# Block 2 of a two-block cross-attention kernel: keys and values from split operands, a later output product, and a second set of banks for some pairs

## What is computed

```python
# block 1
x1 = layernorm(x + mha(x, x, Wq1, Wk1, Wv1, causal=True))        # keys past a counted length are masked
x2 = layernorm(x1 + mha(x1, context, Wq2, Wk2, Wv2, causal=False))
h  = layernorm(x2 + (relu(x2 @ fc1_w.T + fc1_b) @ fc2_w.T + fc2_b))
# block 2
q, k, v = h @ wq + bq, context @ wk + bk, context @ wv + bv      # 16 heads of 64
scores = q @ k.T / 8 + fside + fside                             # fside: (32, 16, 64, 64)
out = layernorm(softmax(scores) @ v @ wo + bo + h)
```

## Time and profile before

| | |
|---|---|
| time, median of 3 runs | 393.7 us (392.85 to 400.62) |
| the profiled execution | 397.58 us |
| its span, first to last instruction | 395.4 us |
| mean granted TensorE clock | 0.956 |
| TensorE matmul busy | 345.0 us (87%) |
| VectorE / ScalarE / GpSimd busy | 293.4 / 232.7 / 235.7 us |
| DMA | 17.86 MB, mean 45 GB/s |

### The profile page before, as it was taken

One profiled execution on the slowest core, in us unless ns is written; L12 is line 12 of the kernel. 1 busy time (PEld: TensorE's weight loads), 2 busy tenths in 40 slices (PEclk: granted clock), 3 DMA queues, 4 the chain that ended last, 5 costly groups with the idle time before them and its releaser, 6 DMA issues.

```text
span 395.4 us, 13051 instructions
## 1 busy us (share of the span) xinstructions
PE 345.0 (87%) x5296; PEld 240.2 (61%) x5296; DVE 293.4 (74%) x833; ACT 232.7 (59%) x561; POOL 235.7 (60%) x372
## 2 busy tenths in 40 slices
PE   2868979899999999999999999999999978776644
PEld 1434535658686868585858586868675747364533
DVE  3554793897989898979797989797979675735141
ACT  1314625485858686767677676768685837363421
POOL 0135161658485858585858585858686665665361
PEclk9968889999999999999999999999999999999955
DMA  5991000010001010102020202020202020101000
GB/s 163 325 342 48 0 2 2 2 55 3 2 2 61 5 61 3 61 2 61 5 61 4 61 2 61 5 61 2 61 5 61 2 61 2 61 2 61 8 8 7
DMA packets 13178, 17.86 MB, mean 45 GB/s; under 512 B 1600, under 2 KB 10176, under 8 KB 13120
## 3 DMA queue, kind: packets, MB, share of 16 engines
q1 hardware_dynamic: 13120, 17.04, 13.9%
HBM read 15.99 MB, written 1.05 MB: 43 GB/s over the span
## 4 chain that ended last, share of the span: by engine, by line
PE 73%; POOL 8%; DVE 7%; ACT 6%; issue 4%; DMA 1%; SPq 1%; POOLq 0%; ACTq 0%; DVEq 0%
PE C_E L455 8%; PE C_E L537 7%; PE C_E L488 6%; PE C_E L469 6%; PE C_E L514 4%; PE C_E L528 4%; PE A_E L365 4%; PE C_E L503 3%; PE B_E L365 3%; PE A_E L398 2%; PE B_E L398 2%; PE B_E L384 2%; POOL B_kblk L888 2%; PE B_X L384 2%; PE A_X L384 2%
## 5 line engine op out<-in xcount | busy, mean ns | idle before, releaser
L568 ACT ACTIVATE A_S<-A_S 128x512 f32<-128x512 f32 x32 | 20.2, 631 | 65.8 <-DVE A_S L766 65.8
L888 POOL TENSOR_TENSOR A_kblk<-A_qk,cst 128x1024 f32<-128x1024 f32 x16 | 30.4, 1898 | 41.1 <-DVE A_qk L734 39.8
L896 POOL TENSOR_TENSOR L_ve<-L_mv,cst 128x1 f32<-128x1 f32 x64 | 12.3, 192 | 61.4 <-DVE L_mv L799 61.3
L929 POOL TENSOR_TENSOR Sc<-Sc,mxc 128x512 f32<-128x512 f32 x32 | 33.4, 1044 | 22.2 <-DVE mxc L846 22.2
L907 POOL TENSOR_TENSOR L_xg<-L_xh,vec_sb 128x128 f32<-128x128 f32 x64 | 29.4, 459 | 17.9 <-DVE L_xh L808 17.9
L898 POOL TENSOR_TENSOR L_rstd<-L_ve,cst 128x1 f32<-128x1 f32 x64 | 35.2, 551 | 5.0
L537 PEld LDWEIGHTS C_E<-wo_sb,C_zT 128*128 128x128 f32 x256 | 31.4, 200 | 11.1 <-ACT C_zT L633 11.1
L537 PE MATMUL C_E<-wo_sb,C_zT 128*128 128x128 f32 x256 | 34.6, 291 | 3.5 <-ACT C_zT L633 3.5
L455 PE MATMUL C_E<-cTs,wk_sb 128*128 128x512 f32 x64 | 36.0, 645 | 0.3 <-DVE Sc L837 0.3
L938 POOL TENSOR_TENSOR Pc<-Pc,rdc 128x512 f32<-128x512 f32 x32 | 33.0, 1045 | 4.8 <-DVE rdc L856 4.8
L646 ACT ACTIVATE qT<-C_E,bq 128x128 f32<-128x128 f32 x128 | 34.8, 384 | 0.7 <-PE C_E L488 0.7
(11 more groups left out here) (148 smaller groups left out, 954.5 us busy)
## 6 DMA issues: line engine op xcount, KB each, us to landing
f<-in_fs SPq DMA_DIRECT2D x16, 512.0 KB, 4.1
out<-osb SPq DMA_DIRECT2D x16, 64.0 KB, 2.0
xTs<-in_xT SPq DMA_DIRECT2D x1, 768.0 KB, 8.7
xs<-in_x SPq DMA_DIRECT2D x1, 768.0 KB, 10.7
cs<-in_ctxn SPq DMA_DIRECT2D x1, 768.0 KB, 12.4
cTs<-in_ctxT SPq DMA_DIRECT2D x1, 768.0 KB, 9.8
vec_sb<-in_vecs SPq DMA_DIRECT2D x1, 640.0 KB, 6.9
wk_sb<-in_wk SPq DMA_DIRECT2D x1, 512.0 KB, 4.3
```

What stands on the lines that cost most here:

```text
L888: tt(a.kblk[:], a.qk[:, 1].unsqueeze(1).to_broadcast([P, 8, P]), at["rmask"].unsqueeze(2).to_broadcast([P, 8, P]), ALU.mult).then_inc(a.s_ ...
L929: tt(v, v, mxc[:, 8 * g:8 * g + 8].unsqueeze(2).to_broadcast([P, 8, S]), ALU.subtract).then_inc(C.s_sub, 1)
```

## The change

1. **Split keys, values.** The context (`cT_hi`, `cT_lo`, for four pairs at a time) and the weights (`wk_hi`, `wk_lo`, `wv_hi`, `wv_lo`) are split: `hi` is a copy in the type F32R, `lo` is what is left. Keys and values are each three products with F32R operands in place of the f32 ones: hi by hi, lo by hi, hi by lo. The values are now two products' worth of 512 columns over all 128 tokens of the pair, and no longer go by sequence. New steps make the halves: `C.whi`, `C.wvhi`, `C.chi` on ScalarE, `C.wlo`, `C.wvlo` on VectorE, `C.clo` on GpSimd.
2. **Scores and bias.** In `C.e` the bank now goes by sequence `b`, and the partition half by `hl ^ b`. The bias arrives sorted to match (`by_half`, on the host), and `C.fadd_g` adds it once, reading four head pairs across both banks. The factor 2 moves: queries are scaled by half (`QSCALE`), and exp has `scale=2.0`.
3. **Delayed output product.** `C.o` is one step and comes after the next pair's scores and their sum with the bias. `C.e` waits for the copies `C.zts` of the pair before it and no longer for `C.y`.
4. **Two places.** From pair 12 (`SPLIT`) the odd pairs of block 2 use the E and X banks of chain A, which has then done its last pair, and its buffers. `place(n)` gives the set, `before(n)` the pair that had it before.
5. **Blank products.** `idle_products` multiplies zeros (bf16, 512 columns) into B's X bank: 7 at the start, 2 in each of 16 steps `K.warm` ahead of B's first scores, 3 in each of 16 steps `L.warm` after B's last norm, the last seven of these after the last output product.
6. **Order.** `MOVES` gives each step of each pair a shift of its own, so that periods need no longer have one order. In the middle the order on TensorE is, for example: `C.pt`(3) `A.qkv`(9) `C.zt`(3) `B.e`(6) `B.f1`(5) `C.e`(4) `A.pt`(8) `C.o`(3) `B.pt`(6) `C.k`(8) `C.v`(5) `B.tr`(7) `C.x3t`(5) `C.q`(5) `A.e`(9). Before it was `C.pt`(3) `C.zt`(3) `A.e`(8) `C.o`(3) `A.qkv`(9) `C.e`(4) `B.e`(6). The first order on ScalarE is `A.qk`(0) `C.whi`(0) `A.exp_0`(0). At the end TensorE has `C.x3t`(15) `C.q`(15) `C.pt`(14) `C.e`(15) `C.zt`(14), four blank steps, `C.o`(14), then `C.pt`(15), `C.zt`(15) and `C.o`(15) with three blank steps between them, and seven more.
7. The GpSimd step `gb` also waits for its own instruction of the pair before.

```diff
+QSCALE = 0.5 * float(DK1) ** -0.5
...
+def by_half(fs):
+    f = fs.reshape(PAIRS, 2, J, 2, S, S)
+    halves = [np.stack([f[:, b, :, c ^ b] for b in range(2)], axis=2) for c in range(2)]
+    return np.stack(halves, axis=1).transpose(0, 1, 4, 2, 3, 5).reshape(B * S, H * S)
...
-            a.J, a.E, a.X = ps(name + "_J"), ps(name + "_E"), ps(name + "_X")
+            a.J, a.EE = ps(name + "_J"), ps(name + "_E", 2)
+            a.E, a.X = a.EE[:, 0:HALF], a.EE[:, HALF:2 * HALF]
...
-        C.E = [ps("C_E0"), ps("C_E1")]
+        C.EE = ps("C_E", 2)
...
+        cT_hi, cT_lo = ([sb(f"{n}{k}", [P, FIRST * P], F32R) for k in range(2)] for n in ("cT_hi", "cT_lo"))
+        wk_hi, wk_lo, wv_hi, wv_lo = (sb(n, [P, HD], F32R) for n in ("wk_hi", "wk_lo", "wv_hi", "wv_lo"))
...
+        own = [Chain(), Chain()]
+        for k, o in enumerate(own):
+            o.EE = (C.EE, A.EE)[k]
+            o.E = [o.EE[:, b * HALF:(b + 1) * HALF] for b in range(2)]
+            o.S = A.S if k else sb("Sc", [P, H * S])
+            o.P = A.S if k else sb("Pc", [P, H * S])
+            o.PT = A.PT if k else sb("PTc", [P, H * S])
+            o.qT = A.kblk if k else sb("qT", [P, J, P])
+            o.zT = (wk_sb if k else sb("C_zT", [P, HD]))[:].rearrange("p (j b c) -> p j b c", b=2, c=S)
+            o.x3T = sb(f"x3T{k}", [P, P])
+            o.mx, o.den, o.rd = (sb(f"C_{nm}{k}", [P, H]) for nm in ("mx", "den", "rd"))
+
+        def place(n):
+            return own[n % 2 if n >= SPLIT else 0]
+
+        def before(n):
+            if n <= SPLIT:
+                return n - 1
+            return n - 2 if n > SPLIT + 1 else -1
...
+            def idle_products(to, count):
+                for _ in range(count):
+                    last = mm(to, blank[:, 0:P], blank[:], start=True, stop=True)
+                return last
+
+            def warm_first(n):
+                idle_products(Bc.X[:, :], 2).then_inc(warmed, 1)
+
+            def warm_last(n):
+                pe.wait_ge(L2.s_xh, PAIRS)
+                idle_products(Bc.X[:, :], 3)
...
+                    if a is Bc and n == 0:
+                        pe.wait_ge(warmed, PAIRS)
...
                     group, j = n // FIRST, 2 * (n % FIRST) + g
-                    if j < 2 and group < 2:
-                        pe.wait_ge(s_cT[group], 16)
+                    if j == 0:
+                        pe.wait_ge(C.s_clo, group + 1)
                     if n == 0:
-                        pe.wait_ge(w_keys, 16 * 3)
+                        pe.wait_ge(C.s_wlo, 1)
                     elif n < FIRST:
                         pe.wait_ge(C.s_ks, 2 * n - 1 + g)
                     else:
-                        pe.wait_ge(C.s_s, 2 * (n - FIRST) + 1 + g)
-                    mm(C.E[g][:, :], wk_sb[:, j * P:(j + 1) * P], cTs[:, group * FIRST * P:(group + 1) * FIRST * P],
-                       start=True, stop=True).then_inc(C.s_k, 1)
-                return step
-
-            def c_v(b):
+                        pe.wait_ge(C.s_s, 2 * (n - FIRST) + 2)
+                        if g == 0 and before(n - FIRST) >= 0:
+                            pe.wait_ge(L4.s_y, before(n - FIRST) + 1)
+                    hi, lo = (w[:, j * P:(j + 1) * P] for w in (wk_hi, wk_lo))
+                    chi, clo = cT_hi[group % 2], cT_lo[group % 2]
+                    to = place(max(n - FIRST, 0)).E[g]
+                    mm(to, hi, chi[:], start=True, stop=False)
+                    mm(to, lo, chi[:], start=False, stop=False)
+                    mm(to, hi, clo[:], start=False, stop=True).then_inc(C.s_k, 1)
+                return step
+
+            def c_v(m):
 
                 def step(n):
                     if n + 3 < PAIRS:
-                        pe.wait_ge(C.s_ks, 2 * (n + 3) + 1 + b)
+                        pe.wait_ge(C.s_ks, 2 * (n + 3) + 1 + m)
                     else:
-                        pe.wait_ge(C.s_s, 2 * n - 1 + b)
+                        pe.wait_ge(C.s_s, 2 * n)
+                        if m == 0 and n - 1 <= SPLIT:
+                            pe.wait_ge(L4.s_y, n - 1)
                     if n == 0:
-                        pe.wait_ge(w_values, 16 * 2)
-                    for r in range(2):
-                        last = mm(C.E[b][S * r:S * r + S, :], cTs[:, n * P + S * b:n * P + S * b + S], wv_sb[:, r],
-                                  start=True, stop=True)
-                    last.then_inc(C.s_v, 1)
+                        pe.wait_ge(C.s_wlo, 2)
+                    chi, clo = (c[n // FIRST % 2][:, n % FIRST * P:(n % FIRST + 1) * P] for c in (cT_hi, cT_lo))
+                    hi, lo = (w[:, m * HALF:(m + 1) * HALF] for w in (wv_hi, wv_lo))
+                    to = place(max(n - 1, 0)).E[m]
+                    mm(to, chi, hi, start=True, stop=False)
+                    mm(to, chi, lo, start=False, stop=False)
+                    mm(to, clo, hi, start=False, stop=True).then_inc(C.s_v, 1)
...
-                pe.wait_ge(C.s_vs, 2 * n + 2)
+                if n <= SPLIT:
+                    pe.wait_ge(C.s_vs, 2 * n + 2)
+                elif n == SPLIT + 1:
+                    pe.wait_ge(L1.s_xh, PAIRS)
+                else:
+                    pe.wait_ge(L4.s_y, n - 1)
                 if n == 0:
                     pe.wait_ge(bvo_ready, 2)
-                tr(C.E[0][:, 0:P], h2[n % RING][:], ident).then_inc(C.s_x3t, 1)
+                tr(place(n).E[0][:, 0:P], h2[n % RING][:], ident).then_inc(C.s_x3t, 1)
...
                 pe.wait_ge(C.s_qs, 2 * n + 2)
-                if n:
-                    pe.wait_ge(L4.s_y, n)
+                if before(n) >= 0:
+                    pe.wait_ge(C.s_zts, 2 * before(n) + 2)
+                o = place(n)
                 pe.wait_ge(C.s_ks, 2 * FIRST * (n // FIRST) + 2 * FIRST)
...
-                            last = mm(C.E[hl][S * b:S * b + S, j * S:(j + 1) * S], qT[r, j, S * b:S * b + S],
+                            last = mm(o.E[b][S * (hl ^ b):S * (hl ^ b) + S, j * S:(j + 1) * S], o.qT[r, j, S * b:S * b + S],
                                       keys[r, j, S * b:S * b + S], start=True, stop=True)
...
                     pe.wait_ge(C.s_nrm, 2 * n + 1 + g)
-                    pe.wait_ge(C.s_qs, min(2 * n + 4, 2 * PAIRS))
+                    if n < SPLIT:
+                        pe.wait_ge(C.s_qs, 2 * n + 4)
+                    elif n + 1 < PAIRS:
+                        pe.wait_ge(C.s_vs, 2 * n + 4)
+                    if n == SPLIT:
+                        pe.wait_ge(L4.s_y, n)
...
                 pe.wait_ge(C.s_pts, 2 * n + 2)
-                for jj in range(J // 2):
-                    for b in range(2):
-                        c = jj * P + S * b
-                        for hl in range(2):
-                            for r in range(2):
-                                k = slice(S * r, S * r + S)
-                                v = jj * P + DK1 * hl
-                                last = mm(C.E[r][DK1 * hl:DK1 * hl + DK1, c:c + S], V[n % 2][k, b, v:v + DK1],
-                                          PTc[k, hl * HALF + c:hl * HALF + c + S], start=True, stop=True)
+                pe.wait_ge(C.s_vs, 2 * n + 2)
+                o = place(n)
+                for j in range(J):
+                    for hl in range(2):
+                        for b in range(2):
+                            r, v, c = slice(S * b, S * b + S), (2 * j + hl) * DK1, j * P + S * (hl ^ b)
+                            last = mm(o.E[b][DK1 * hl:DK1 * hl + DK1, j * S:(j + 1) * S], V[n % 2][r, v:v + DK1],
+                                      o.PT[r, c:c + S], start=True, stop=True)
                 last.then_inc(C.s_zt, 1)
 
-            def c_o(r):
-
-                def step(n):
-                    pe.wait_ge(C.s_zts, 2 * n + 1 + r)
-                    for jj in range(J // 2):
-                        last = mm(C.E[0][:, 0:D], zT[:, r, jj], wo_sb[:, 2 * jj + r], start=(r == jj == 0),
-                                  stop=(r == 1 and jj == J // 2 - 1))
-                    last.then_inc(C.s_o, 1)
-                return step
-
-            steps = {"B.tr": b_tr, "B.f1": f1, "B.f2": f2, "B.f3": f3, "C.x3t": c_x3t, "C.e": c_e, "C.zt": c_zt, "C.bvo": bvo,
+            def c_o(n):
+
+                pe.wait_ge(C.s_zts, 2 * n + 2)
+                if n < SPLIT:
+                    pe.wait_ge(C.s_s, 2 * n + 4)
+                for j in range(J):
+                    last = mm(place(n).E[0][:, 0:D], place(n).zT[:, j].rearrange("p b c -> p (b c)"), wo_sb[:, j],
+                              start=(j == 0), stop=(j == J - 1))
+                last.then_inc(C.s_o, 1)
...
+            pe.wait_ge(blank_ready, 1)
+            idle_products(Bc.X[:, :], 7)
...
+            def whi(n):
+                if n:
+                    return
+                act.wait_ge(w_keys, 16 * 3)
+                act.copy(wk_hi[:], wk_sb[:]).then_inc(C.s_whi, 1)
+
+            def wvhi(n):
+                if n:
+                    return
```

(47 more changed lines are left out.)

578 lines of the change are left out of this document (507 added, 71 removed).

## The result

The changed kernel takes 379.87 us (median of 4 runs, 379.01 to 380.16) against 393.79 for the kernel before on the same chip: 0.960 of the time, interval 0.955 to 0.965. It is faster by 4%: 13.9 us less, where the forecast of 358 had 35.8 less, so it is 22 us above the forecast, just inside the stated range of 342 to 380. Some executions of one kernel run about 2% longer at a lower granted clock than the rest; every ratio here is of executions outside that state. The profiled execution has a span of 378.1 us against 395.4. Of these 17.3 us some 3.4 are no gain of the change: the profiled execution of before was 3.8 us above its median, that of after is at its median.

A forecast was written before the change was run, and what follows sets the result against it. In the middle only TensorE's work was taken to count. Span 395.4 less 12.5 (middle), 17.2 (drain) and 6.0 (start) gave 359.7; plus 2.2, less 3.9, forecast 358 us, range 342 to 380.

The forecast's parts named there:

- The middle, -12.5: Eleven steady periods: split keys and values save 1.14 us a pair on TensorE, period 20.06 to 18.92, 12.5 us in all.
- The first rival: Middle: VectorE's waits on block 1 hand-overs stay, VectorE sets a period of 20, the 12.5 us are gone: 370.5; chance 0.15.
- What hides the split: Copies on ScalarE and subtractions on GpSimd stay covered in the period; uncovered they would cost 6.5 us in all.
- That rival: Score products: two row halves in one bank take turns, the 1.09 us double, 16 us more: 374; chance 0.05.
- the F32R rivals: Key and value products: two passes, 394, chance 0.06; the f32 price, 466, chance 0.04; a price between, 0.01.
- Drain, -17.2: End of the span after the middle: four stretches between landmarks, (a) to (d), together save 17.2 us.
- (a): Drain, second attention's scores of pair 13 to pair 15, 38.8 us: rounds shorten to 17.5 and 15, -6.3 us.
- (b): Drain, scores of pair 15 to the transposition of block 2's input: 25.0 us becomes 22, -3 us.
- (c): Drain, that transposition to block 2's scores, 10.3 us: with its own banks pair 15 waits only for pair 13's copy, -4.7 us.
- (d): Drain, last scores to the end, 21.3 us: blank steps and pair 14's products keep the upper clock level, -3.2 us.
- Start, -6.0: First 75 us: clock gains of 3.2 and 2, 3 more, less 1 for blank products and 1.2 for a later first exp.
- 3 more: Start, 51.74 to the next scores at 74.64: 22.9 us against 20.06 later, with waits for data; 3 us saved.

The follow-up runs named there:

- f32_keys_values: Kernel after with one f32 product for each key and value step in place of three F32R ones, splitting steps kept: 388.29 us, ratio 0.985.
- old_order_all: Split, scores by sequence and delayed output product put in the periodic order of the kernel before, without blank products or second place: 502.18 us, ratio 1.265.
- short_den: Kernel after with block 2's softmax denominator summed over 8 of its 64 columns: 378.75 us, ratio 0.961.
- short_maximum: Kernel after with the two maxima of block 2's scores taken over 8 of 64 columns: 378.19 us, ratio 0.953.
- hi_only_clean: Kernel after with only the hi by hi key and value products, and without the subtractions that make the low parts: 376.24 us.
- hi_only: Kernel after with only the hi by hi product in each key and value step, the two corrections left out: 377.13 us, ratio 0.958.
- no_blanks: Kernel after without all blank products and the waits on them: 382.24 us, ratio 0.969.
- before_short_maximum: Kernel before with the maxima of block 2's scores over 8 of 64 columns, all products kept: 397.57 us, one run.

## Why the prediction was wrong, point by point

**The middle, -12.5: wrong, and the main miss (10.9 of 18.4 us of span).** Three things failed in it. The step that fell is "so in the middle only TensorE's own work counts", with VectorE at 18.6, "late next, by a margin of 0.3 us", as the sole floor. TensorE's 20.02 busy of 20.06 was no proof of slack elsewhere: the runs with fewer columns, which change nothing but the price of these products, both stop at 19.69, though the second spares TensorE more than the 1.14 forecast. The rest of the forecast's 1.14 could not be had. I had looked for the next limit in the waits of one engine (1.5 us of VectorE's idle time); but what the runs show in its place are loops of hand-overs through several engines, of 19.6 to 19.7 us.

Second, the price: 0.23 a product with 0.31 to 0.34 for the first of a group makes 3.15 a pair, not 2.64: the term left out what the first of a group takes. One pass was right.

Third, the forecast charged the rest of the change nothing in the middle; it costs 0.56 a period, which the split (0.59) just pays back. Of this, 0.26 is more idle time of TensorE (five periods of `f32_keys_values`: 101.67 busy of 103.15) and 0.31 is TensorE busy 20.33 a period instead of 20.02. Start to start, the query products take 1.97 us for 1.79 and the scores 1.09 for 0.98, while keys and values take 3.57, less than before's 3.79, now that the values are whole products; why the others got longer stays open, and so does whether the old order could carry the split, since `old_order_all` has other troubles.

The first rival, "the middle doesn't speed up", came true for this part. Its reason, hand-overs that leave VectorE to set a period of 20, did not: `short_den` and `short_maximum` take 0.9 us a pair off VectorE and the period moves by 0.05 at most.

**What hides the split, strided add, scores.** Held: the copies and subtractions are covered in the middle (`hi_only_clean`, without the subtractions, has the period of `hi_only`), and the score product's 64 records take 1.16 us in the timelines of both kernels, so the overlap of the row halves survives in one bank (the 1.09 of rows 3 is from the view of the chain). That rival is out, and the F32R rivals with it. The strided sum takes 0.68 us, as before.

**Drain, -17.2: -13.1.** (a) failed: -0.3 for -6.3. The step "the second goes to 15, between 13.4 and 15.82" took TensorE's busy time for the limit again; `hi_only` has 38.47 for this stretch with eight products a pair less. After's chain there:

```profile
310.31 0.60 DVE C_den L955
...
314.11 1.91 POOL B_kblk L989
...
316.06 1.13 PE B_E L407 x8
```

Block 2's denominators on VectorE and a norm on GpSimd stand ahead of the second attention's key blocks. Nothing tried in this order shortened the stretch by more than 1.1 us: 37.80 with short maxima (37.38 with one product besides), 38.04 with short denominators, but also 37.79 without blank products. (b) came out at -3.5 for -3, (c) at -6.2 for -4.7 and (d) at -2.5 for -3.2, in the way foretold: the last scores wait for the copy of their queries alone ([0.50 <-ACT A_kblk L731] above; `A_kblk` holds pair 15's queries) and go after 4.1 us, and the blank products bring the last output product from 3.8 us back to 2. Another 0.5 was gained between the last A.e and pair 13's scores.

**Start, -6.0: -2.6 to pair 4** (-3.9 to pair 5, where one period of 18.8 follows). The stall on the keys' weights is there as foretold:

```profile
16.13 1.05 ACT L675 CAST wk_hi<-wk_sb 128x1024 fp32r<-128x1024 f32 x1 [8.69 <-DMA bq_sb<-in_bq]
17.09 0.63 ACT L632 ACTIVATE A_S<-A_S 128x512 f32<-128x512 f32 x1
```

The first exp starts at 17.09 instead of 16.03. What I over-counted are gains of the clock in the first rounds (three scores, 3.2 us; A.e of pair 3 comes 1.1 earlier) and the 2 and "3 more" up to pair 4 (1.5 together; for the 3 there was no row that tied it to the clock or to a wait). The step that failed is that blank products are needed to hold the clock up there: `no_blanks` comes to pair 4 only 0.3 us later. And even the 2.6 may not belong to the change. `before_short_maximum`, in the order of before and without blank products, has its A.e of pair 4 at 71.64, against 74.64 in the profiled execution of before; from 36 to 50 us its granted clock is 1.00, and 0.76 in the other. So the kernel before can have such a start too, and one profiled execution of each can't say how often.

**The sum.** The span is 18.4 us above the forecast, 10.9 from the middle, 4.1 from the drain and 3.4 from the start. The last 3.5 of the 22 come from the step between span and time: the forecast took 3.9 us off because before's profiled execution was that much slower than its median, and after's profiled execution has no such excess to take off. The result stayed within 342 to 380 by the width of the range, not by its reasons.

## What to carry to other kernels

An engine that is busy all the time bounds the kernel, but its busy time doesn't say how far the others are behind: shrink one of its steps in the unchanged kernel and see where the period stops, before pricing the rest. In this order, in which TensorE was full, several loops of hand-overs end just under its time; 0.9 or 1.8 us less TensorE work gave 0.37 us. The drain, where one chain is nearly alone, paid 13.1 of the 17.3 us of span, and was forecast to within 1.5 us wherever the next wait was named. And read two executions of the unchanged kernel before a gain of 3 us at one end is put down to the change.

## What the hardware showed that I had not expected

- An F32R product of 512 columns takes 0.23 us from start to start at a granted clock of 1.00, the first of a group mostly 0.31 to 0.34, where an f32 product takes 0.86.
- The granted clock at both ends differs from one kernel to the next though the work there is nearly the same: from 36 to 50 us 0.76 in the kernel before and 1.00 in `before_short_maximum`; from 334 to 354 us 1.00 in both, and 0.83 to 0.91 in all four kernels with fewer columns; from 354 to 374 us 1.00 before and 0.74 to 0.83 in the other five. With one profiled execution of each, why it fell isn't settled.
- At the lower clock level the last output product takes 3.8 us, and with blank products ahead of it 2.05.
- The two row halves of the score product write to one bank on different partitions without losing their overlap: 64 records in 1.16 us, as before.
